# Cross-attention and quantised feed-forward: the output projection from fp16 parts instead of fp32r parts

## The reference

```python
x = x + xattn(layernorm(x), ctx, ctx, Wq, Wo)     # Q, K and V all by Wq; out @ Wo.T
x = x + ffn(layernorm(x))
# xattn: softmax(Q K^T / sqrt(32)) V, per head, then the output projection by Wo
# ffn: activations and weights rounded to 8-bit steps:
#   gate, up = xq @ w_gate_q.T, xq @ w_up_q.T;  h = silu(gate) * up
#   quantise(h) @ w_down_q.T
```

## Time and profile before

| | |
|---|---|
| median of 3 runs | 1085.98 us (1085.36 to 1088.84) |
| the profiled execution | 1086.07 us |
| its span | 1083.8 us |
| mean granted TensorE clock | 0.992 |
| PE busy over the span | 1049.3 us (97%) |
| DVE busy | 857.0 us (79%) |
| ACT busy | 752.1 us (69%) |
| POOL busy | 532.3 us (49%) |

### The profile page before, as it was taken

One profiled execution on the slowest core, in us unless ns is written; L12 is line 12 of the kernel. 1 busy time (PEld: TensorE's weight loads), 2 busy tenths in 40 slices (PEclk: granted clock), 3 DMA queues, 4 the chain that ended last, 5 costly groups with the idle time before them and its releaser, 6 DMA issues. The chain is left out here.

```text
span 1083.8 us, 18315 instructions
## 1 busy us (share of the span) xinstructions
PE 1049.3 (97%) x6391; PEld 617.6 (57%) x6421; DVE 857.0 (79%) x1426; ACT 752.1 (69%) x905; POOL 532.3 (49%) x445
## 2 busy tenths in 40 slices
PE   8779999999999999999998899999999999999998
PEld 6646666767776667777754544444444444344444
DVE  5888989899888898777767778777777877777576
ACT  4577888888888888888777375666657564875550
POOL 5878877798777887677552000000000000386485
PEclk9989999999999999999999999999999999999999
DMA  7434667667655555652147356767673313899995
GB/s 248 137 98 122 186 186 186 194 184 207 172 164 175 169 176 159 189 152 74 68 153 231 108 205 223 253 213 262 214 245 96 112 25 97 343 415 426 425 398 223
DMA packets 121609, 214.40 MB, mean 198 GB/s; under 512 B 59056, under 2 KB 68144, under 8 KB 110384
## 3 DMA queue, kind: packets, MB, share of 16 engines
q1 hardware_dynamic: 118640, 184.41, 52.9%
q10 hardware_dynamic: 2880, 28.84, 6.4%
HBM read 134.26 MB, written 66.75 MB: 185 GB/s over the span
## 5 line engine op out<-in xcount | busy, mean ns | idle before, releaser
L1324 POOL TENSOR_TENSOR x<-x,c_y 128x512 f32<-128x512 f32 x32 | 53.8, 1714 | 365.9 <-DVE c_y L1368 348.6
L1096 ACT ACTIVATE e_sg<-e_G,x_gus 128x512 f32<-128x512 f32 x176 | 119.1, 685 | 114.5 <-PE e_G L1208 110.7
L961 PE MATMUL a_Q<-a_xT,wq 128*128 128x512 f32 x732 | 186.4, 403 | 1.2 <-DVE wq L663 1.2
L1168 DVE SCALAR_TENSOR_TENSOR h<-e_U,x_gus,e_sg 128x512 f32<-128x512 f32 x176 | 131.9, 749 | 69.8 <-PE e_U L1212 40.8
L504 POOL TENSOR_TENSOR a_pl<-a_pr,a_ph 77x1024 f16<-77x1024 f32 x60 | 129.0, 2150 | 113.4 <-DVE a_pl L730 73.7
L1208 PE MATMUL e_G<-e_cT,gu 128*128 128x512 bf16 x690 | 178.8, 379 | 0.7
L1212 PE MATMUL e_U<-e_cT,gu 128*128 128x512 bf16 x689 | 178.6, 379 | 0.7
L918 PE MATMUL a_O<-a_wo,a_aT 128*128 128x512 f32 x720 | 176.8, 395 | 0.6 <-POOL a_aT L494 0.6
L961 PEld LDWEIGHTS a_Q<-a_xT,wq 128*128 128x128 f32 x732 | 134.0, 190 | 47.6 <-issue 19.1
L569 ACT ACTIVATE a_pr<-a_S,a_ebias 77x2048 f32<-77x2048 f32 x64 | 125.9, 1967 | 45.3 <-PE a_S L941 43.6
L918 PEld LDWEIGHTS a_O<-a_wo,a_aT 128*128 128x128 f32 x720 | 133.4, 189 | 28.8 <-issue 3.3
(11 more groups left out here) (188 smaller groups left out, 1547.7 us busy)
## 6 DMA issues: line engine op xcount, KB each, us to landing
x<-x_d SPq DMA_DIRECT2D x24, 1024.0 KB, 6.3
h_d<-h SPq DMA_DIRECT2D x20, 1024.0 KB, 4.1
a_xr<-in_x SPq DMA_DIRECT2D x64, 256.0 KB, 3.5
a_xt<-in_xT SPq DMA_DIRECT2D x64, 256.0 KB, 3.8
x_d<-a_xr SPq DMA_DIRECT2D x64, 256.0 KB, 2.5
a_xs<-in_x SPq DMA_DIRECT2D x60, 256.0 KB, 3.8
h<-h_d ACTq DMA_DIRECT2D x10, 1536.0 KB, 24.5
h<-h_d ACTq DMA_DIRECT2D x10, 1280.0 KB, 27.7
```

The lines of the kernel that those rows point to most:

```text
L961: mm = nc.tensor.matmul(q_bank(n.n)[:], wq[:, wp, j, P * n.g:P * (n.g + 1)], xT[:, n.par, xp, j], start=(ins == 0), stop=(ins == 3 * KT - 1))
L1096: nc.scalar.activation(sg[:, s], G[:, t % GU], ACT.Silu, scale=gus[:, t:t + 1]).then_inc(silued, 1)
L1168: nc.vector.scalar_tensor_tensor(out=h[:, place(u, p), t], in0=U[:, t % GU], scalar=gus[:, IT + t:IT + t + 1], in1=sg[:, s], op0=ALU.mult, ...
```

## The change

`wo` and `aT` become fp16, again in a high and a low part. To fit, Wo is divided by a scale, one for the whole matrix: `osc` is the greatest magnitude of Wo times `sv`, divided by 2^14. What was multiplied by `sv` in L752 goes into Wo instead: Wo is multiplied by `ws = sv / osc`. The projection then comes out as the true value over `osc`, and the residual x is brought to the same scale before the sum: POOL multiplies the tile in `xr` by `ob = 1 / osc`, in place, in slot k for item k-6, behind its half of `pl` and the spreading of keys, and before the weight cast. The sum L791 then multiplies by `osc` where it multiplied by 1.0.

For the scale DVE takes the row maxima of Wo in slots -2 to 1; PE transposes the column of 128 maxima in slot 2, DVE reduces it in slot 3. The high parts of `wo` are made by ACT in slots 3 to 6, the low parts by DVE in slots 4 to 7. Wo's fp32 copy keeps a buffer of its own, so the first loads of feed-forward weights no longer wait for the low parts. Buffers are padded so that the others keep their places. A semaphore `scales` takes the place of `iv_rdy`, `pro_turned` of `wsum`, and `consts` counts what `mx_zero` did.

```diff
-        wo = sb("a_wo", [P, 2, KT, D], F32R)
+        wo = sb("a_wo", [P, 2, KT, D], F16)
+        wo32 = sb("a_wo32", [P, KT, D])
-        aT = sb("a_aT", [P, 2, 2, KT, TOK], F32R)
+        aT = sb("a_aT", [P, 2, 2, KT, TOK], F16)
@@ sync @@
-                    if w.i < 2:
-                        sp.wait_ge(wo_lo, KT)
-                    else:
+                    if w.i >= 2:
@@ gpsimd @@
-                        nc.gpsimd.tensor_tensor(aT[:, n.par, 1, n.g], att[:], aT[:, n.par, 0, n.g].bitcast(F32),
-                                                ALU.subtract).then_inc(aT_l, 1)
+                        nc.gpsimd.tensor_tensor(aT[:, n.par, 1, n.g], att[:], aT[:, n.par, 0, n.g], ALU.subtract).then_inc(aT_l, 1)
...
-                    if 0 <= k < KT:
-                        pool.wait_ge(wo_hi, k + 1)
-                        nc.gpsimd.tensor_tensor(wo[:, 1, k], wo32[:, k], wo[:, 0, k].bitcast(F32), ALU.subtract).then_inc(wo_lo, 1)
...
+                    if (n := at(k, -6)):
+                        if n.n == 0:
+                            pool.wait_ge(statted, TT)
+                            pool.wait_ge(scales, 4)
+                        pool.wait_ge(xr_in[n.g], 16 * (n.block + 1))
+                        nc.gpsimd.tensor_scalar(xr[:, n.g], xr[:, n.g], ob[:, 0:1], None, ALU.mult).then_inc(xr_scaled, 1)
@@ scalar @@
-                    if -1 <= k < KT - 1:
-                        act.wait_ge(w_in, 16)
-                        nc.scalar.activation(wo[:, 0, k + 1], wo32[:, k + 1], ACT.Copy).then_inc(wo_hi, 1)
+                    if 0 <= (j := k - WO_FROM) < KT:
+                        act.wait_ge(scales, 4)
+                        nc.scalar.activation(wo[:, 0, j], wo32[:, j], ACT.Copy, scale=ws[:, 0:1]).then_inc(wo_hi, 1)
@@ vector @@
-                        nc.vector.reciprocal(iv[:], sv[:]).then_inc(iv_rdy, 1)
+                        nc.vector.reciprocal(iv[:], sv[:]).then_inc(scales, 1)
+                        nc.vector.tensor_tensor(wsv[:], wtop[:], sv[:], ALU.mult).then_inc(scales, 1)
+                    if k == WO_FROM:
+
+                        dve.wait_ge(pro_turned, 2)
+                        nc.vector.tensor_reduce(gtop[:], O[:, 0:P], AX.X, ALU.max).then_inc(scales, 1)
+                        dve.wait_ge(scales, 3)
+                        own.step(nc.vector.tensor_scalar(osc[:], gtop[:], 0.5 ** WO_BITS, 1.0e-30, ALU.mult, ALU.max))
+                        own.step(nc.vector.reciprocal(ob[:], osc[:]))
+                        nc.vector.tensor_tensor(ws[:], sv[:], ob[:], ALU.mult).then_inc(scales, 1)
+                    if 0 <= (j := k - WO_FROM - 1) < KT:
+                        dve.wait_ge(wo_hi, j + 1)
+                        nc.vector.scalar_tensor_tensor(out=wo[:, 1, j], in0=wo32[:, j], scalar=ws[:, 0:1], in1=wo[:, 0, j],
+                                                       op0=ALU.mult, op1=ALU.subtract).then_inc(wo_lo, 1)
...
-                        nc.vector.scalar_tensor_tensor(out=att[:], in0=A[:], scalar=sv[:, 0:1], in1=rcp[:],
-                                                       op0=ALU.mult, op1=ALU.mult).then_inc(att_rdy, 1)
+                        nc.vector.tensor_tensor(att[:], A[:], rcp[:], ALU.mult).then_inc(att_rdy, 1)
...
+                    if -2 <= k < KT - 2:
+                        if k == -2:
+                            dve.wait_ge(w_in, 16)
+                        own.step(nc.vector.tensor_reduce(wm[:, k + 2:k + 3], wo32[:, k + 2], AX.X, ALU.max, apply_absolute_value=True))
+                        if k == KT - 3:
+                            own.step(nc.vector.tensor_reduce(wtop[:], wm[:], AX.X, ALU.max))
...
                         dve.wait_ge(projected, n.n + 1)
-                        dve.wait_ge(xr_in[n.g], 16 * (n.block + 1))
+                        dve.wait_ge(xr_scaled, n.n + 1)
                         t = xr[:, n.g]
                         nc.vector.memset(hold[:], 0.0)
-                        nc.vector.tensor_tensor_reduce(t, projection(n), t, 1.0, -3.0e38, ALU.add, ALU.max,
+                        nc.vector.tensor_tensor_reduce(t, projection(n), t, osc[:, 0:1], -3.0e38, ALU.add, ALU.max,
                                                        mom[:, n.block, n.g, 2:3]).then_inc(x1_rdy, 1)
@@ tensor @@
+                def turn_wo():
+
+                    pe.wait_ge(scales, 2)
+                    nc.tensor.transpose(O[:, 0:P], wsv[:].to_broadcast([P, P]), id32[:]).then_inc(pro_turned, 1)
```

More of the change, by code:

```diff
@@ L179 @@
 V_SLOTS = (2, 3, 4, 6)
+WO_FROM, WO_BITS = 3, 14
 SQ = 32
@@ L236, in attend @@
             ks = tmp("p_ks", [P, GROUPS, NK])
-        aT = sb("a_aT", [P, 2, 2, KT, TOK], F32R)
+        aT = sb("a_aT", [P, 2, 2, KT, TOK], F16)
+        sb("a_pad0", [P, D])
+        sb("a_pad", [P, 2048])
+        wm = sb("a_wm", [P, KT])
+        wtop, wsv, gtop, osc, ob, ws = (sb("a_" + n, [P, 1]) for n in ("wtop", "wsv", "gtop", "osc", "ob", "ws"))
+        sb("a_pad2", [P, 2 * KT * TOK - D - 2048 - KT - 6])
         pr = sb("a_pr", [KEYS, HG, TOK])
@@ L258, in attend @@
         esig = sb("a_esig", [P, 2])
-        with ExitStack() as pro:
-            wo32 = pro.enter_context(nc.sbuf_tensor("p_wo32", [P, KT, D], F32))
         wraw = sb("w_raw", [P, 2, D])
@@ L298, in attend @@
         xl_own, xr0_rdy, k32_rdy = sem("a_xl_own"), sem("a_xr0_rdy"), sem("a_k32_rdy")
-        ph_a, ph_b, pl_a, pl_b, v_hi, v_lo, iv_rdy, k_scaled, rt_rdy, own_p = (sem("a_" + n) for n in (
-            "ph_a", "ph_b", "pl_a", "pl_b", "v_hi", "v_lo", "iv_rdy", "k_scaled", "rt_rdy", "own_p"))
+        ph_a, ph_b, pl_a, pl_b, v_hi, v_lo, scales, k_scaled, rt_rdy, own_p = (sem("a_" + n) for n in (
+            "ph_a", "ph_b", "pl_a", "pl_b", "v_hi", "v_lo", "scales", "k_scaled", "rt_rdy", "own_p"))
         w_measured, w_scaled, w_coded, w_cast = (sem("w_" + n) for n in ("measured", "scaled", "coded", "cast"))
-        (w_in, c_in, wo_hi, wo_lo, consts, mx_zero, statted, r0_rdy, rs_rdy, rs_out, r_turned, rsb_rdy,
+        (w_in, c_in, wo_hi, wo_lo, consts, xr_scaled, statted, r0_rdy, rs_rdy, rs_out, r_turned, rsb_rdy,
          xT_h, xT_l, q_done, q_scaled, qT_h, qT_l, scored, m_scored, maxed, m_turned, mT_rdy, exped,
-         summed, valued, ln_done, rcp_rdy, att_rdy, aT_h, aT_l, projected, x1_rdy, mom_rdy, wsum, centred,
+         summed, valued, ln_done, rcp_rdy, att_rdy, aT_h, aT_l, projected, x1_rdy, mom_rdy, pro_turned, centred,
          wc_hi, wc_lo, own_d, own_a) = (sem("a_" + n) for n in (
-             "w_in", "c_in", "wo_hi", "wo_lo", "consts", "mx_zero", "statted", "r0_rdy", "rs_rdy", "rs_out", "r_turned", "rsb_rdy",
+             "w_in", "c_in", "wo_hi", "wo_lo", "consts", "xr_scaled", "statted", "r0_rdy", "rs_rdy", "rs_out", "r_turned", "rsb_rdy",
              "xT_h", "xT_l", "q_done", "q_scaled", "qT_h", "qT_l", "scored", "m_scored", "maxed", "m_turned", "mT_rdy", "exped",
-             "summed", "valued", "ln_done", "rcp_rdy", "att_rdy", "aT_h", "aT_l", "projected", "x1_rdy", "mom_rdy", "wsum", "centred",
+             "summed", "valued", "ln_done", "rcp_rdy", "att_rdy", "aT_h", "aT_l", "projected", "x1_rdy", "mom_rdy", "pro_turned", "centred",
              "wc_hi", "wc_lo", "own_d", "own_a"))
@@ L475, in _ @@
                 nc.gpsimd.memset(epsb[:], EPS).then_inc(consts, 1)
-                nc.gpsimd.memset(mx[:], 0.0).then_inc(mx_zero, 1)
+                nc.gpsimd.memset(mx[:], 0.0).then_inc(consts, 1)
                 nc.gpsimd.memset(ones[:], 1.0).then_inc(consts, 1)
@@ L576, in _ @@
                     if k == V_SLOTS[0]:
-                        act.wait_ge(iv_rdy, 1)
+                        act.wait_ge(scales, 1)
                         nc.scalar.activation(ks[:], k32[:], ACT.Copy, scale=iv[:, 0:1]).then_inc(k_scaled, 1)
@@ L682, in _ @@
                     if k == -6:
-                        dve.wait_ge(wsum, 1)
+                        dve.wait_ge(pro_turned, 1)
                         for j in range(KT):
@@ L742, in _ @@
                         if n.n == 0:
-                            dve.wait_ge(mx_zero, 1)
+                            dve.wait_ge(consts, 3)
                         after(dve, m_turned, n.block)
@@ L760, in _ @@
                             dve.wait_ge(aT_h, STEPS)
-                            nc.vector.tensor_tensor(aT[:, done.par, 1, done.g], att[:], aT[:, done.par, 0, done.g].bitcast(F32),
-                                                    ALU.subtract).then_inc(aT_l, 1)
+                            nc.vector.tensor_tensor(aT[:, done.par, 1, done.g], att[:], aT[:, done.par, 0, done.g], ALU.subtract).then_inc(aT_l, 1)
                     if k in V_SLOTS:
@@ L803, in sum_w @@
                     if j == KT - 1:
-                        mm.then_inc(wsum, 1)
+                        mm.then_inc(pro_turned, 1)
                 def project_k(g, j):
@@ L832, in project_v @@
                     after(pe, v_lo, b)
+                    if b == 1:
+                        pe.wait_ge(scales, 3)
```

(4 more changed lines are left out.)

## The result

The changed kernel takes 1112.68 us (median of 4 runs, 1112.56 to 1113.93) against 1086.24 us for the kernel before (1085.36 to 1088.84): ratio 1.0239, 95% interval 1.0227 to 1.0252. It is slower by 26.4 us where 39 were forecast; the time lies inside the stated range and 0.7 us above the stated lower edge of the main case.

The account below looks back on a forecast made before the run. PE sets the pace before; after the change, POOL's operations plus DVE's half of the low probabilities were to overfill the slot. 1086.07 + 38.4 (stage) + 4 (beginning) - 3 (tail) = 1125.5, said as 1125 us; range 1097 to 1142.

Parts of the forecast that it names:

- stated range: Whole kernel: 8 in 10 that the time falls between 1097 and 1142 us.
- main case: Whole kernel: POOL's overfull ring slows the attention stage; 1125 us, own range 1112 to 1142, chance 0.71.
- The circle: Attention slots: POOL's operations plus DVE's half of the low probabilities must fit a slot; 8.54 us after the change.
- DVE's turn: Attention slots: DVE's half of the low probabilities and POOL exclude each other; 1.10 us a slot, between 0.98 and 1.22.
- Rival (c): Attention slots: DVE's half and POOL overlap more, so its turn costs nothing; about 1083 us, chance 0.07.
- The size: Slots 6 to 56: 51 x 8.54 plus casts, key spreads and root work make 481.8 us, +38.4.
- every slot's circle is at least PE's slot: Attention stage: each slot's ring is at least PE's 8.3 us, so light slots do not make up for heavy ones.
- (a): POOL's scaling costs what a two-tensor operation costs, 1.25 us; kernel 1107 us, chance 0.13.
- (b): POOL's scaling runs at the cast's rate, 0.57 us, and PE's saving comes through; kernel 1080 us, chance 0.09.
- PE's saving: Output projection on PE: 12 matmuls at 0.216 instead of 0.238 us, about 0.25 us a slot.
- The beginning: First slots: DVE's added maxima and low parts of Wo, partly hidden by idle time; +4 us, between 0 and 9.
- The tail: From slot 57 POOL has less work and PE's 0.25 us comes through in some 12 slots; -3 us.

Follow-up runs that it names:

- run 3: Kernel before, with only POOL's in-place multiplication of x added at its new place, by a factor of 1: 1119.31 us, ratio 1.0296.
- run 1: Changed kernel with POOL's scaling of x left out, so the residual stays unscaled: 1080.5 us, ratio 0.9938 to the kernel before.
- run 6: Changed kernel with POOL's scaling of x placed ahead of its half of the low probabilities instead of behind it: 1112.87 us, ratio 1.0249 to the kernel before.
- run 7: Changed kernel with DVE's half of the low probabilities replaced by an equally long one-operand maximum with a small result: 1085.81 us, ratio 0.9989 to the kernel before.
- Run 4: Changed kernel with POOL scaling only 256 of the 512 columns of x: 1088.51 us, ratio 1.0013 to the kernel before.
- run 2: Changed kernel with the scaling of x moved from POOL to ACT: 1081.83 us, ratio 0.9949 to the kernel before.
- run 5: Changed kernel without any global scale: fp16 parts only, factor kept in DVE's product, no maxima, no scaling of x: 1079.87 us, ratio 0.9933 to the kernel before.

## Why the prediction was right

**The circle.** The step on which the forecast rested, that POOL's operations and DVE's half of the low probabilities form a closed circle that the earlier trace rows show full at 8.72 us, holds: run 3 has the loss without the rest of the change, run 1 the change without the loss, run 6 that the place is indifferent, run 7 that DVE's turn is part of it. Rival (c), that they overlap after all, is refuted by run 7 beside the changed kernel. Run 4 shows that what stays under PE's pace costs little and what is over it costs its excess.

**The size.** The mechanism was right and its size half again too large: the stage was forecast at +38.4 and came to +26.1. The terms were too high on the same side, each once per slot. The scaling stands in the order from 275.03 to 276.55, 1.52 us, where 1.62 was taken: 51 x 0.10 = 5 us. The low part of qT with DVE's turn takes 2.25 where 1.29 + 1.10 = 2.39 was taken: 7 us. Of these 5 are DVE's turn, 1.0 (2.29 less 1.29), taken between 0.98 and 1.22; 2 come from 1.29 being a duration where POOL's steps from start to start are 1.25. The fp16 low part of the attended values saves 0.13 instead of 0.10 (1.16 against 1.29): 1.5 us. With these the plain circle is 2.12 + 1.52 + 1.25 + 1.12 + 2.25 = 8.26 us, which is what POOL takes in the eleven plain slots from 29 to 55 (8.25 to 8.28). 51 x 8.26 + 46.3 = 467.6 us, measured 469.6. The 2 us more lie in slots 6 and 7, where POOL goes from L506 to L506 in 11.31 and 10.55 us instead of 9.83 for a slot with cast and spreading; before the next L506 it stands 1.9 and 1.2 us.

The prediction also held that every slot's circle is at least PE's slot. That failed narrowly: in plain slots PE has no wait and goes from scores to scores in 8.41 us, while POOL, with no gap either, goes in 8.27.

```profile
354.29 0.94 PE L966 MATMUL a_S<-a_qT,a_kt 32*77 32x512 f32 x12 [0.60 <-DVE a_mx L763]
...
362.70 0.93 PE L966 MATMUL a_S<-a_qT,a_kt 32*77 32x512 f32 x12
```

So POOL makes up a little, about 0.14 us a slot, of what the heavy slots put it behind.

The stated lower edge of the main case does not follow from its own terms: 1.5 for the scaling is 6 us less, 0.95 for the turn 8 less and nothing at the beginning 4 less, which makes 1108 us, not 1112. By that sum the measured 1112.68 lies less close to the edge than it seems.

**Rivals (a) and (b)** hung on the price of the scalar form. At 1.56 us it is neither the two-operand form's 1.29 nor the cast's 0.60. The rule that one-input work on GpSimd runs near line rate (the Trainium skill, GPSIMD Engine Reference, Engine selection) does not hold for this form here; the row of L481, at 308 columns, was the right guide.

**PE's saving** was taken as 0.25 us a slot and is 0.14. The pitch of 0.216 was right for fp16, but 0.238 was no pitch: it is 2.86 divided by 12, and contains the 0.33 us from the last matmul to the scores that fp16 hardly shortens. From start to start the matmuls before took 0.230. In the changed kernel this hid behind POOL; in runs 1, 2 and 5 it is why they gain 5 to 7 us. Rival (b)'s 1080 us agrees with the 1080.5 of run 1 by luck: it gave 0.25 us to 29 slots, where run 1 has 0.14 in nearly all 51.

**The beginning** was forecast at +4, and slot 6 opens 1.6 us later. One term in it was too low: DVE's four low parts of Wo take 2.54, 1.53, 0.85 and 2.23 us, 7.2 together, where 2.7 to 4.8 was taken, and yet slot 6 opens only so much later. The tail was forecast at -3 and came to -1.1; 12 slots at 0.14 would be -1.7. That SP's edits cost nothing is borne out: POOL waits for an x to arrive three times, 5.3 us together over the whole program, and not once from 84 to 520 us. On DVE the sum with its factor in SBUF takes 0.74 us instead of 0.69, which the prediction left out, and the attended values 0.67 instead of 0.73.

**What was to be seen**, point by point: POOL busy over 8 in each 9 us, yes (79.2 in 80); 9.1 us with a cast, 8.84; over 10 with key spreading, from slot 20 on 9.8 to 10.1, and 10.7 and 11.2 where the reciprocal root comes in the same slot; 8.6 in plain slots, POOL 8.27 and PE 8.41; PE at about 90%, 92%; L748 near 2 us in most slots, mean 1.96; the projection in 2.6 us, 2.69; the scaling at 1.6, 1.56. Waits of L897 or L569 on L504 exist (3.4 and 13.8 us), but the prediction did not see that most of PE's wait would be put down to DVE's maxima.

## What to carry to other kernels

An engine that is 80% busy may have no room at all: add up, for a slot, its own instructions and those of the other engine that it must take turns with and wait for, and compare that circle with the pace of the bound engine. Before putting an operation on the idle-looking engine, look for a slot in which the trace already has an operation of such a length too many; here the key-spreading slots gave the direction without a run. And a time divided by the number of instructions is no pitch when it contains the change to the next group: take the pitch from start to start. A table of waits names the last in a row, here DVE's maxima, not the one that made them late.

## What the runs showed of the hardware

GpSimd's tensor_scalar on fp32 with its factor in SBUF takes 0.92 us for 128x256 and 1.56 for 128x512: 2.5 ns a column and 0.28 us fixed. Those two put L481's 308 columns at 1.05, which is what it takes. The two-operand form is cheaper at 512 columns (1.29 us, 1.16 with an fp16 result and operand).

GpSimd's strictly ordered queue does not keep DVE out: a two-operand DVE instruction that stands while a POOL operation runs gets its turn before POOL's next one: L500 stands in the order at 279.49 with no gap before it and takes 2.29 us instead of 1.29.

In this stage a 128x128 by 512 matmul goes every 0.230 us from fp32r operands and every 0.217 from fp16 ones; from bf16 ones in the feed-forward it is 0.215. The last one before the scores takes 0.31 to 0.33 us from its start to theirs.
